# Two packed attentions: fills, weight splitting and small work moved between engines, terms spread out when stored

## The reference

```
l0x: norm(x); k, v from the context (masked rows), q from x; 8 heads of 16; 256 keys
     softmax(q k^T / 4 + mask) v, projected together with norm(x), added to x
l1x: norm(x); q, k, v from x; context rows are further keys and values
     16 heads of 8; 512 keys (256 of the context, 256 of x), projected, added to x
```

## Time and profile before

| | us |
|---|---|
| three runs | 1285.53, 1290.31, 1293.37 |
| median | 1290.31 |
| the profiled execution | 1288.04 |
| its span | 1286.2 |

### The profile page before, as it was taken

The page is one execution under the profiler, slowest core; times in us unless marked ns, Lnnn a source line. Parts: engine busy times, 40 slices in busy tenths (PEclk is TensorE's granted clock), DMA queues, the critical chain, the costliest instruction groups (busy, mean ns, idle before and its releaser), DMA issues.

```text
span 1286.2 us, 18277 instructions
## 1 busy us (share of the span) xinstructions
PE 1104.2 (86%) x6234; PEld 778.7 (61%) x6234; DVE 812.3 (63%) x1962; ACT 676.8 (53%) x1601; POOL 406.6 (32%) x576
## 2 busy tenths in 40 slices
PE   3587899999739998778989999967999799998777
PEld 2346677777513444656667777745777567675665
DVE  6865687888668783577766776665211366666464
ACT  2154566676414556366767787752333256666022
POOL 7401111111530000235556776673100144444200
PEclk8598899999967999898989999986999899999979
DMA  5301000000022400300000000305000100000000
GB/s 208 99 27 55 1 1 1 1 1 1 1 82 61 169 21 1 132 0 1 1 1 1 1 1 1 131 18 218 1 1 1 67 1 2 1 2 1 1 1 18
DMA packets 24733, 42.75 MB, mean 33 GB/s; under 512 B 3616, under 2 KB 22336, under 8 KB 23360
## 3 DMA queue, kind: packets, MB, share of 16 engines
q1 hardware_dynamic: 24640, 41.58, 9.2%
HBM read 36.94 MB, written 4.46 MB: 32 GB/s over the span
## 4 chain that ended last, share of the span: by engine, by line
PE 68%; DVE 15%; ACT 8%; issue 3%; POOL 2%; SPq 2%; DMA 1%; DVEq 0%; ACTq 0%; POOLq 0%
PE psum L1071 7%; PE psum L1442 7%; PE psum L1061 5%; PE psum L813 5%; PE psum L823 4%; ACT region_d L1508 4%; PE psum L346 3%; PE psum L2075 3%; PE psum L2052 2%; PE psum L1429 2%; PE psum L319 2%; PE psum L2019 2%; PE psum L2036 2%; PE psum L2014 2%; PE psum L1479 2%
## 5 line engine op out<-in xcount | busy, mean ns | idle before, releaser
L1442 PE MATMUL psum<-gated_parts 128*128 128x512 f32 x768 | 198.4, 413 | 16.6 <-DVE region_d L1613 15.7
L1442 PEld LDWEIGHTS psum<-gated_parts 128*128 128x128 f32 x768 | 142.6, 193 | 68.3 <-DVE region_d L1613 33.0
L1682 POOL TENSOR_TENSOR region_d<-region_d 128x256 f32<-128x256 f32 x128 | 101.8, 796 | 119.0 <-DVE region_d L1613 117.6
L1146 ACT ACTIVATE rounds_work<-psum,region_c 128x512 f32<-128x512 f32 x128 | 86.9, 689 | 59.8 <-PE psum L1061 59.8
L132 POOL TENSOR_TENSOR rstd<-var_eps,minus_half 128x4 f32<-128x4 f32 x16 | 16.3, 1020 | 282.8 <-DVE var_eps L92 280.7
L1613 DVE SCALAR_TENSOR_TENSOR region_d<-psum,ctx,region_d 128x128 f32<-128x128 f32 x256 | 71.8, 344 | 43.1 <-ACT region_d L1508 39.6
L1508 ACT ACTIVATE region_d<-psum,gated_work 128x128 f32<-128x128 f32 x256 | 75.1, 439 | 44.9 <-issue 26.2
L1071 PE MATMUL psum<-parts,split 128*128 128x512 f32 x384 | 97.8, 404 | 0.0
L1061 PE MATMUL psum<-parts,split 128*128 128x512 f32 x384 | 94.7, 397 | 0.0
L675 DVE TENSOR_REDUCE work<-psum 128x1 f32<-128x512 f32 x128 | 82.3, 684 | 18.5 <-PE psum L308 17.7
L1302 POOL CAST parts<-rounds_work 128x1024 fp32r<-128x1024 f32 x32 | 33.3, 1041 | 183.9 <-ACT rounds_work L1146 183.9
(11 more groups left out here) (377 smaller groups left out, 2318.1 us busy)
## 6 DMA issues: line engine op xcount, KB each, us to landing
region_a<-in_l1v SPq DMA_DIRECT2D x1, 4096.0 KB, 15.1
region_b_last<-in_l1o SPq DMA_DIRECT2D x1, 4096.0 KB, 12.0
region_a<-in_l2f SPq DMA_DIRECT2D x1, 4096.0 KB, 13.7
region_b_last<-in_l3f_small SPq DMA_DIRECT2D x1, 4096.0 KB, 19.8
region_a<-in_l3f SPq DMA_DIRECT2D x1, 2080.0 KB, 7.7
region_c<-in_l0f SPq DMA_DIRECT2D x1, 2076.0 KB, 12.1
region_c<-in_l3x SPq DMA_DIRECT2D x1, 2048.0 KB, 7.7
front_work<-q_parts SPq DMA_DIRECT2D x24, 64.0 KB
```

The costliest lines, as they stand in the source:

```text
L1146: act.activation(H[g % 2][:, f, :], bank[f], ACT.Gelu_apprx_tanh, bias=W("b1")[:, (g % E) * FT + f:(g % E) * FT + f + 1]).then_inc(h_ready ...
L1442: ins = pe.matmul(bank[2 * (n % 2) + c], src[a][:, t * P:(t + 1) * P], weights[b][:, piece(c)], start=m == 0, stop=m == len(PASSES) - 1)
L1682: pool.tensor_tensor(tile[:, 0:2, :], tile[:, 0:2, :], tile[:, 2:4, :], ALU.add).then_inc(k.pool_chain, 1)
```

## The change

Seven edits. (1) l1x: POOL no longer fills slots ahead of the norm; the key slots are filled with ones during l0f (two bfloat16 ones written as one float32 word), queries not at all, `VA` after the splitting of q and k. (2) l0x: fills in words, one memset for a slot pair. (3) l0x: the splitting of l0f's weights waits for `z_ready` (after step 4) where it waited for `rest`. (4) Stores write every part to each block that uses it, 12 DMAs for a half where there were 6; a load is one DMA for keys and one for queries. With heads of 8 the stack has 48 rows, not 96. (5) l0x: the masks are sent before the stores; the context parts go out in 6 DMAs, not 3. (6) l1x: the maxima are copied by ACT and split by four POOL instructions; the output copies and the values of x go to ACT, those of the context to POOL; both stages: ACT takes the maxima ahead of the exponential of its step. (7) In l1x ACT waits for all stores before its loop, as in l0x.

```diff
+ONES_16 = float(np.array([0x3F803F80], np.uint32).view(np.float32)[0])
-    R_MASK = 96
+    R_MASK = len(TERMS) * HD
...
+        act.wait_ge(*stored.at(16 * 24))
         for i in range(ALL + LAG + 1):
             s = i - LAG
+            if i % SU == 0 and 0 < i <= ALL:
+                maxima(i // SU - 1)
             if 0 <= s < ALL:
...
-            if masked and s > 0 and s % key_tiles == 0:
+            if s > 0 and s % key_tiles == 0:
...
+            if not masked and i % STEPS == VALUES_AT % STEPS and VALUES_AT <= i < ALL + VALUES_AT:
+                own_values((i - VALUES_AT) // STEPS)
...
         if masked:
             ahead.pool_consts(pool)
-            fill_queries(0)
+            pool.memset(slot_words[0], ONES_16).then_inc(fill_done.semaphore, 1)
             k.norm.gpsimd(pool, use)
             k.prepare_mask(pool)
-            for i in range(BUFS):
-                if i > 0:
-                    fill_queries(i)
-                pool.memset(KS[i][:, :, :], 1.0).then_inc(fill_done.semaphore, 1)
+            for i in range(1, BUFS):
+                pool.memset(slot_words[i], ONES_16).then_inc(fill_done.semaphore, 1)
         else:
-            fill_queries(0)
-            fill_queries(1)
-            pool.memset(KS[0][:, :, :], 1.0).then_inc(fill_done.semaphore, 1)
             k.norm.gpsimd(pool, use)
-            pool.memset(KS[1][:, :, :], 1.0)
+            pool.wait_ge(*rest.at(8))
...
-            pool.wait_ge(*rest.at(8))
+            pool.wait_ge(ahead.z_ready, 2)
             split.gpsimd(pool)
+            return
+
+        def split_maxima(v):
+            pool.wait_ge(*nm_part.at(v + 1))
...
+            pool.tensor_copy(high, f).then_inc(nm_rest.semaphore, 1)
+            pool.wait_ge(*nm_rest.at(3 * v + 1))
+            chained(pool.tensor_tensor(r, f, high, ALU.subtract))
+            pool.tensor_copy(mid, r).then_inc(nm_rest.semaphore, 1)
+            pool.wait_ge(*nm_rest.at(3 * v + 2))
+            pool.tensor_tensor(low, r, mid, ALU.subtract).then_inc(nm_rest.semaphore, 1)
...
-                    sp.dma_start(by_part(dram[PIECES[m][0]], i)[:, :, cols], parts[i][:, cols])\
-                        .then_inc(stored.semaphore, 16)
+                    dram, places = (k_dram, K_ROWS) if PIECES[m][0] == "k" else (q_dram, Q_ROWS)
+                    for row in places[i]:
+                        store(dram, NH, parts[i], row, cols).then_inc(stored.semaphore, 16)
...
             load_keys(k_dram, b, NK - S, share)
-            for r, (i, _) in enumerate(TERMS):
-                sp.dma_start(QS[b % BUFS][r * HD:(r + 1) * HD, heads, :], rows_of(q_dram, i, 1, b)[:, heads, :])\
-                    .then_inc(done, 16)
+            sp.dma_start(QS[b % BUFS][0:R_MASK, heads, :], rows_of(q_dram, heads, b)).then_inc(done, 16)
...
+            if FILL_AT <= g < FILL_AT + 4:
+                n = g - FILL_AT
+                pool.memset(k.later_slots[n // 2][:, n % 2 * REGION_B // 4:(n % 2 + 1) * REGION_B // 4], ONES_16)\
+                    .then_inc(k.slots_filled.semaphore, 1)
```

More of the change, by code:

```diff
@@ L179, in packed_attention @@
     k.carve_from(0)
-    QS = [k.carve(BF16, NH, S) for _ in range(BUFS)]
-    KS = [k.carve(BF16, NH, NK) for _ in range(BUFS)]
+    QS, KS, slot_words = [], [], []
+    for i in range(BUFS):
+        first = k.carve_mark()
+        if masked:
+            QS.append(k.carve(BF16, NH, S))
+        KS.append(k.carve(BF16, NH, NK))
+        slot_words.append(k.work[:, first:k.carve_mark()])
+    if not masked:
+        QS = [k.carve(BF16, NH, S) for _ in range(BUFS)]
+        k.later_slots = slot_words
     VA = [k.carve(F32, key_tiles, NH, SLOT) for _ in range(2)]
@@ L185, in packed_attention @@
     NMp = [[k.carve(BF16, P) for _ in range(3)] for _ in range(2)]
+    NMf = [k.carve(F32, P) for _ in range(2)]
     vtmp = k.carve(F32, HALF)
@@ L342, in weighted_values @@
                 pe.wait_ge(*v_sb.at(b + 1))
+                if not masked:
+                    pe.wait_ge(*ctx_values.at(b + 1))
             if kt == 0 and g >= 1:
@@ L458, in scalar @@
                                ACT.Copy).then_inc(av_out.semaphore, 1)
[L459 to L465, removed]
+            if masked and i % SU == 1 and SU < i <= ALL + 1:
                 v = i // SU - 1
@@ new lines, in gpsimd, with store @@
+        for i in range(ALL + VALUES_AT):
+            if i % SU == 0 and 0 < i <= ALL:
+                split_maxima(i // SU - 1)
+            if i % STEPS == VALUES_AT % STEPS and VALUES_AT <= i < ALL + VALUES_AT:
+                values_of_ctx((i - VALUES_AT) // STEPS)
+    def sync(sp):
+        def store(dram, heads, part, row, cols):
+            return sp.dma_start(dram.rearrange("(h r d) t -> r h d t", h=heads, r=len(TERMS))[row, :, :, cols],
+                                part[:, cols])
+        Q_ROWS = [[r for r, term in enumerate(TERMS) if term[0] == i] for i in range(3)]
+        K_ROWS = [[r for r, term in enumerate(TERMS) if term[1] == i] for i in range(3)]
@@ L595, in sync @@
             for i in range(3):
-                if i < 2:
+                if not masked:
+                    sp.wait_ge(*nm_rest.at(3 * v + i + 1))
+                elif i < 2:
                     sp.wait_ge(*nm_part.at(2 * v + i + 1))
@@ L606, in sync @@
                     sp.wait_ge(*ready)
-                    sp.dma_start(k.c_dram.rearrange("(h i d) t -> i h d t", h=16, i=3)[i], cp[i]).then_inc(c_stored, 16)
+                    for row in K_ROWS[i]:
+                        store(k.c_dram, 16, cp[i], row, slice(0, T)).then_inc(c_stored, 16)
         if masked:
@@ L647, in values @@
             if b == 0:
-                dve.wait_ge(*fill_done.at(BUFS + 1 if masked else 2))
+                dve.wait_ge(*fill_done.at(BUFS + 1))
             if b >= 2:
                 dve.wait_ge(*av_done.at(STEPS * (b - 1)))
[L651 to L667, removed]
-                                          bank[7][:, t * P:(t + 1) * P].rearrange("p (h d) -> p h d", h=NH))
+            tmp = vtmp[:, 0:TPB * P].rearrange("p (t n) -> p t n", t=TPB)
+            chain.then(dve.tensor_tensor(tmp, bank[7][:, 0:TPB * P].rearrange("p (t n) -> p t n", t=TPB),
+                                         W("bv").unsqueeze(1).broadcast_to([P, TPB, P]), ALU.add))
+            for t in range(TPB):
+                tt = b * TPB + t
+                ins = dve.tensor_scalar(VA[b % 2][:, t, :, 0:HD],
+                                        vtmp[:, t * P:(t + 1) * P].rearrange("p (h d) -> p h d", h=NH),
+                                        k.mask_col[:, tt:tt + 1], None, ALU.mult)
             ins.then_inc(v_sb.semaphore, 1)
@@ L686, in vector @@
                 ahead.dve_rows(dve, chain)
-            if i % SU == 0 and 0 < i <= ALL:
+            if masked and i % SU == 0 and 0 < i <= ALL:
                 v = i // SU - 1
@@ L2798, in loads_of @@
     def loads_of(self, name):
-        return 16 * (len(TERMS) + (3 + 1 if name == "l0x" else 3 + 3))
+        return 16 * 3
     def weight_views(self, name, layout, *more):
```

112 lines of the change are left out of this document (66 added, 46 removed).

## The result

| | us | runs |
|---|---|---|
| before, beside it | 1291.74 median (1285.53 to 1293.37) | 4 |
| after | 1364.24 median (1363.17 to 1366.65) | 4 |
| ratio | 1.057, 95% interval 1.054 to 1.060 | |
| profiled execution after | 1363.7, span 1362.0, mean clock 0.859 | |

Slower by 5.7%, where the prediction had 1275 in a range of 1266 to 1284. Two lines of the page's second part, in 40 slices of the span, show the place: in the kernel before PE's granted clock stands at 8 or 9 tenths from slice 14 on but for dips; here it is at 5 from slice 12 to 17, with PE's busy share at 9 in each.

A forecast was written before the change was run, and what follows sets the result against it. It saw l1x's norm held beside POOL's fills, then a bare chain, DVE in the first 12 steps and mostly PE after. l1x -12.6 and l0x -1.3 gave -13.9: 1274.1 from 1288.04, 1276.4 from the median, called 1275, range 1266 to 1284.

The forecast's parts named there:

- In the steady part a plain step is 1.56: l1x's steady part: a plain step takes 1.56 us, but 48 steps take 86.0, 1.79 each.
- norm; stores and loads: Head of l1x: norm freed of POOL's fills, -11.8; more stores but fewer loads, net +1.9.
- first pass to the second turn: l1x, start of second pass: less DVE work and no DMA wait, table load partly offsetting: -0.6 (-1.3 to +0.7).
- six units of steps: l1x, steady steps: output copy moved to ACT recovers part of PE's 4.3 us wait: -3.0 (0 to -4.3).
- from the last turn: l1x, last 12 steps, where ACT is the bound: three copies between exponentials, 0.3 each: +0.9.
- head: l0x, head: first pass later behind stores, but PE's sums start at 49.4 for 53.73: -4.3 (-7 to -2).
- moved split, in the steps: l0x, steps 5 to 8: POOL's 13.7 us weight split delays three DVE instructions by 1.65 each: +5.0.
- ACT's order: l0x: taking the maxima ahead of the exponential recovers part of L690's 4.1 us wait: -2.5 (0 to -4).
- context parts, end of stage: l0x: context parts in six DMAs send the last maxima out later: +0.5.
- The reading without that rule: l0x, moved split: without the port-lock rule only wide DVE instructions suffer, making the split's term +1.7.
- the upper prices: Rival, 25%: split holds all five DVE instructions (+6.7), or doubled stores bind in both heads (+3 and +3): 1281.
- POOL's chain: Rival, 6%: in each l1x unit, four POOL maxima pieces exceed the 3.7 us available; at 1.7 each, 1299.

The follow-up runs named there:

- e1: Kernel before with one size changed, the second attention's 48 empty rows removed (48 and 51 rows for 96 and 99): 1372.66 us, ratio 1.060 to 1.066.
- e4: Changed kernel with l1x's rows padded back to 96 and l0x's later-weight split on POOL back at its old place: 1274.84 us, ratio 0.986 to 0.991.
- e10: e4 with POOL's fills of l1x's key slots put back into its norm, one ahead of the power, one behind: 1278.72 us, ratio 0.988 to 0.992.
- e12: Kernel before with one wait changed: l0x's later-weight split on POOL waits for the statistics row, as in the change: 1288.96 us, ratio 0.997 to 1.000.
- e6: e4 with the 48 empty rows zeros instead of ones in the keys' slots: 1275.28 us, ratio 0.987 to 0.991.
- e8: e4 with l0x's six context-part stores put behind the last unit's maxima rows on SP's queue: 1274.66 us, ratio 0.987 to 0.990.
- e11: e4 with l1x's stacks padded to 125 rows and l0x's to 124 (125 with the mask): 1275.29 us, ratio 0.986 to 0.989.

## Why the prediction was wrong

**The step that failed** is the basis of the l1x terms behind the first pass: "In the steady part a plain step is 1.56", with -0.6, -3.0 and +0.9 worked out as if the clock would rise as before. The change's own first line of arithmetic, `R_MASK` from 96 to 48, had no term in the sum and no chance among the rivals. The prediction named it at its very end ("a TensorE clock that stays at its lower level ... now that the contraction is 51 rows and not 99, which nothing in this trace prices") and left the range without it. In e1 it measured +82 us alone, and after, a step took 2.82 where 1.56 was forecast, with the clock at 0.50 and PE busy throughout. A price was at hand, if not a chance: the earlier trace rows shows the lower level, and as an estimate a loss of up to 1.56 us a step over 64 steps is 100 (1.26 was measured, 81 in all). With a chance of even 10% it would have made "slower" 0.14, and the range one-sided where it was symmetric.

**The terms it did have**, read in e4, where the clock is as assumed:

| l1x term | forecast | measured (e4) |
|---|---|---|
| norm; stores and loads (statistics to first pass, 31.78 to 21.50) | -11.8 + 1.9 = -9.9 | -10.3 |
| first pass to the second turn (24.67 to 24.36) | -0.6 | -0.3 |
| six units of steps (86.04 to 82.54) | -3.0 | -3.5 |
| from the last turn (37.28 to 37.28) | +0.9 | 0.0 |
| sum | -12.6 | -14.1 |

These two lines, PE's second and last turn of the maxima in e4, answer the pair in the earlier trace rows:

```profile
395.30 0.27 PE L379 MATMUL psum<-ident,work 128*16 128x128 f32 x1
...
477.84 0.28 PE L379 MATMUL psum<-ident,work 128*16 128x128 f32 x1
```

The norm was right in size, and its reason, DVE's scaling held beside POOL's fills, is borne out by e10; what the 11.8 did not say is that the width of the fills counts beside their place.

| l0x term | forecast | measured |
|---|---|---|
| head | -4.3 | -2.3 (61.81 to 59.48) |
| moved split, in the steps | +5.0 | +4.6 (e12) |
| ACT's order | -2.5 | -0.8 (e4: 27.99 to 27.19) |
| context parts, end of stage | +0.5 | +2.4, with a clock that e1 shows at +3.4 for nothing |
| sum | -1.3 | after: -2.3 + 4.5 + 2.4 = +4.6 |

*Head*: e12, with the old stores, loads and fills, starts its second pass at 55.41; after, at 59.48. The doubled stores are the likely cause of these 4.1, though no run has them alone: ACT's rows landed at 44.9 for a forecast of 42.0, and the first pass began at 36.8 for 34.8. The upper bound that I gave for the landing, 44.5, was about the value. *Moved split*: three instructions of 1.65 were expected on the path. Two of L711 took 2.90 and held PE's turn of the maxima by 3.17, L697 took 2.68 for 1.23, and L742, of only 8 x 128, 0.73 for 0.28. The maxima (L720, from PSUM) took 0.675 beside the split and 0.681 without it, and L707 0.405 in both. The Trainium skill ("SBUF — State Buffer", Who interferes with whom) lets a VectorE instruction with at most one SBUF input pass beside GpSimd unless it is in a two-port mode, counts tensor_scalar among those that can enter such a mode, and holds one with two SBUF inputs against GpSimd's reads. The trace agrees: held are L711, a tensor_scalar, and L697 and L742, with two SBUF inputs each, the small one as well as the wide; L720 and L707, with an input from PSUM, are not. The reading without that rule (+1.7) is out. *ACT's order*: worth a third of the term, if all of e4's gain in the steps is its own.

**The rivals.** None of the four came true as a whole. Of the upper prices, the stores in l0x are true and the split isn't. POOL's chain took 1.62 of the 3.7 us that it had. The rival that should have stood there, "the clock doesn't rise", would not have shown as a wait of PE: PE is busy all the time, and DVE and ACT wait for it.

## What to carry to other kernels

Before matmul rows are cut, to save fills, DMAs or memory, look at the granted clock of that stretch and give the case that it stays low a price and a chance: a lower level can cost up to the whole step again once PE is the bound (1.26 us on 1.56 here). Here 48 idle rows were worth 85 us, and they cost PE no time: two first-pass matmuls take 1.01 with 96 rows and with 48, both at the lower level. The best versions (e4, e6, e8, e11, at 1275) are the change with its rows left in place and the split of l0x where it was. Time an edit to a filler or a layout by itself, as one number in the old kernel (e1), before the rest is built on it. And a stage whose clock falls in a gap, like the end of l0x, can't be read from one profile to better than 3 us.

## What was not expected of the hardware

- With PE busy for 20.00 of 20.00 us, the granted clock stood at 0.50 for some 200 us with contractions of 48 and 51 rows, or of 64 and 67, beside value products of 128 rows; with 96 and 99 rows it was at 1.00 from 390 to 400 us on, with 80 and 83 from 434.7 in the one trace. Rows of zeros counted as rows of ones (1275.28 and 1274.84).
- Few rows in the first pass alone (48, with 99 in the second) held it at 0.50 (1353.18). So did few rows in the second pass (51) once no first pass was left: 0.50 for the last 30 us of the steps, where 99 rows rose after 13.
- More rows than 96 did nothing (1276.27 with 125 and 128).
- POOL fills a slot by 32-bit words in half the time of 16-bit elements: 3.51 for 128x4096, 6.92 for 128x8192, the same bytes.
- The same instructions of l0x ended at 116.58 and at 120.06, with a granted clock of 0.98 and 0.55 in 96 to 104 us.
